# Moving the layer norm's root and two elementwise steps of a cross-attention loop from VectorE to GpSimd, folding the gate into Wo, with a new order of the pieces

## What is computed

```
x1 = x + tanh(g_xattn) * (attention(layernorm(x), ctx) @ Wo + bo)
x2 = layernorm(x1) = (x1 - mean) / sqrt(var + 1e-5)
S  = sigmoid(x2 @ Wg)             # 3584 tokens, 8 experts; each takes its top 896
out = x1 + tanh(g_ffn) * sum over experts of S * (gelu(x2 @ W1 + b1) @ W2 + b2)
```

## Time and profile before

| what | value |
|---|---|
| profiled execution | 894.2 us |
| span | 892.4 us |
| median of three runs | 895.79 us |
| TensorE, VectorE busy | 814.0 us (91%), 708.3 us (79%) |
| ScalarE, GpSimd busy | 571.2 us (64%), 286.0 us (32%) |
| mean granted TensorE clock | 0.961 |

### The profile page before, as it was taken

One profiled execution on the slowest core, in us unless ns is written; L12 is line 12 of the kernel. 1 busy time (PEld: TensorE's weight loads), 2 busy tenths in 40 slices (PEclk: granted clock), 3 DMA queues, 4 the chain that ended last, 5 costly groups with the idle time before them and its releaser, 6 DMA issues. The chain is left out here.

```text
span 892.4 us, 22315 instructions
## 1 busy us (share of the span) xinstructions
PE 814.0 (91%) x8336; PEld 667.8 (75%) x8336; DVE 708.3 (79%) x1900; ACT 571.2 (64%) x1251; POOL 286.0 (32%) x269
## 2 busy tenths in 40 slices
PE   5989999999999999999996118999999999999995
PEld 3555888888888888888775006989898988888885
DVE  6888999999999999999875784787676767764542
ACT  2655877787777777877664214847576675849470
POOL 4760111011111111110100603366465655644504
PEclk9999999999999999999998557999999999999998
DMA  7843666776676676666610304162525344453303
GB/s 190 196 93 89 153 157 153 169 180 155 151 184 152 157 165 165 173 154 150 160 33 29 106 1 134 44 153 50 135 54 136 58 130 102 97 131 67 38 6 41
DMA packets 96210, 104.62 MB, mean 117 GB/s; under 512 B 11744, under 2 KB 92272, under 8 KB 96112
## 3 DMA queue, kind: packets, MB, share of 16 engines
q1 hardware_dynamic: 84128, 88.50, 38.5%
q0 software_dynamic: 10752, 14.69, 9.6%
q10 hardware_dynamic: 1232, 0.12, 0.1%
HBM read 39.60 MB, written 14.68 MB: 61 GB/s over the span
## 5 line engine op out<-in xcount | busy, mean ns | idle before, releaser
L485 DVE TENSOR_REDUCE a_nm<-a_pS 112x1 f32<-112x375 f32 x342 | 177.3, 538 | 4.7 <-PE a_pS L791 4.1
L1772 PE MATMUL e_p<-w2hl,e_hh 128*128 128x512 f32 x440 | 156.9, 397 | 0.0
L725 POOL TENSOR_TENSOR a_kp<-a_k_rest,a_kp 128x375 bf16<-128x375 f32 x56 | 50.4, 900 | 323.7 <-ACT a_kp L326 323.7
L785 PEld LDWEIGHTS a_pT<-a_qst,a_kst 98*128 98x128 bf16 x1536 | 102.8, 99 | 40.8 <-issue 11.7
L785 PE MATMUL a_pT<-a_qst,a_kst 98*128 98x112 bf16 x1536 | 123.5, 212 | 1.7 <-ACT a_P L306 1.0
L1566 POOL DMA_INDIRECT out_dram<-e_y,e_idx x56 | 89.1, 1591 | 109.2 <-ACT e_y L1605 103.2
L1774 PE MATMUL e_p<-w2hl,e_hl 128*128 128x256 f32 x440 | 122.8, 279 | 0.0
L1652 DVE TENSOR_TENSOR e_hl<-e_hid,e_hh 128x384 fp32r<-128x384 f32 (+1 forms) x128 | 77.8, 623 | 47.3 <-ACT e_hh L1598 46.3
L306 ACT ACTIVATE a_room<-a_pT 128x448 f32<-128x448 f32 x192 | 96.7, 543 | 28.1 <-PE a_pT L785 27.8
L791 PE MATMUL a_pS<-a_kst,a_qst 96*112 96x375 bf16 x342 | 107.8, 334 | 3.4 <-DVE a_nm L485 3.0
L306 ACT ACTIVATE a_P<-a_pT 128x448 f32<-128x448 f32 x192 | 97.7, 546 | 9.4 <-PE a_pT L785 8.1
(11 more groups left out here) (247 smaller groups left out, 1688.9 us busy)
## 6 DMA issues: line engine op xcount, KB each, us to landing
a_kst<-a_kp SPq DMA_DIRECT2D x192, 192.0 KB, 3.6
w<-in_L_ffn_W_dram SPq DMA_DIRECT2D x16, 1024.0 KB, 6.8
a_qst<-a_qp SPq DMA_DIRECT2D x96, 112.0 KB, 3.0
a_craw<-in_ctx_dram SPq DMA_DIRECT2D x32, 128.0 KB
a_room<-in_x_dram SPq DMA_DIRECT2D x8, 448.0 KB, 6.6
a_xb<-in_x_dram SPq DMA_DIRECT2D x32, 112.0 KB, 3.4
out_dram<-a_x SPq DMA_DIRECT2D x32, 112.0 KB, 2.2
xn_scratch<-a_x SPq DMA_DIRECT2D x32, 112.0 KB, 2.2
```

Source lines behind the costliest of these rows:

```text
L485: dve.tensor_reduce(nm[:, h:h + 1], s_bank(b, h)[0:LQ, 0:LK], AXX, ALU.max, negate=True).then_inc(s_used, 1)
L785: last = pe.matmul(pT[u % 2][:, j * LQ:(j + 1) * LQ], kst[b % 4][:, h, c * 128:(c + 1) * 128], q_of(b, slice(None), h), start=True, stop=True)
L1772: pe.matmul(p2[g % 2][:], hh[:, f, rows], T.w2hl[r % 2][:, f].rearrange("p q d -> p (q d)"), start=(f == 0), stop=(f == 7), skip_group_che ...
```

## The change

* `added` now adds x plus bias, and writes x1 at once; `gated` is gone. tanh(g) is multiplied once into Wo and into bo, on GpSimd, before the loop.
* GpSimd adds bo to the reloaded x (`x_biased`), one batch ahead of its use; SP reloads x one batch earlier.
* VectorE keeps the statistics of x1 (`x1_statistics`, `x1_moments`). GpSimd takes the inverse root (`root`: a power with exponent -0.5, and two Newton steps, one column each), and the normalised x1 (`x2_of`).
* The bank of the Wo product is free with `x1_ready` instead of `wo_read`.
* The order of the pieces in all loops is new. Both `k_mid_part` of ScalarE are last in the step, the context is loaded for batch m+7 instead of m+8, and the last two key copies of SP stand behind the row of maxima.

```diff
+                dve.wait_ge(xb_ready, b + 1)
                 dve.wait_ge(wo_ready, b + 1)
-                dve.tensor_tensor(xo[:], pM[0][0:LQ, 0:D], bo[:], ALU.add).then_inc(wo_read, 1)
-            def gated(b):
-                dve.scalar_tensor_tensor(xo[:], xo[:], gx[0:LQ], xb[p][:], ALU.mult, ALU.add).then_inc(x1_ready, 1)
+                dve.tensor_tensor(xo[:], pM[0][0:LQ, 0:D], xb[p][:], ALU.add).then_inc(x1_ready, 1)
...
+            def x1_moments(b):
+                dve.wait_ge(ln, b + 1)
+                wait(dve, x2_ready, b - 1)
+                dve.bn_aggr(mv[b % 2][:], stats[:]).then_inc(mv_ready, 1)
...
+            def x_biased(b):
+                pool.wait_ge(xb_loaded[b % 2], 16 * (b // 2 + 1))
+                pool.tensor_tensor(xb[b % 2][:], xb[b % 2][:], bo[:], ALU.add).then_inc(xb_ready, 1)
+
+            def root(b):
+                pool.wait_ge(mv_ready, b + 1)
+                pool.tensor_scalar(ve[:], mv[b % 2][:, 1:2], EPS, None, ALU.add).then_inc(root_set, 1)
+                pool.tensor_scalar(nvh[:], mv[b % 2][:, 1:2], EPS, -0.5, ALU.add, ALU.mult).then_inc(root_set, 1)
+                pool.wait_ge(root_set, 7 * b + 1)
+                pool.tensor_tensor(y[:], ve[:], mhalf[:], ALU.pow).then_inc(root_set, 1)
+                for k in range(2):
+                    pool.wait_ge(root_set, 7 * b + 2 * k + 3)
+                    pool.tensor_scalar(yy[:], y[:], y[:], nvh[:], ALU.mult, ALU.mult).then_inc(root_set, 1)
+                    pool.wait_ge(root_set, 7 * b + 2 * k + 4)
+                    pool.tensor_scalar(y[:], yy[:], 1.5, y[:], ALU.add, ALU.mult).then_inc(root_set, 1)
+
+            def x2_of(b):
+                pool.wait_ge(root_set, 7 * b + 7)
+                pool.tensor_scalar(x2[b % 2][:], x1[b % 2][:], mv[b % 2][:, 0:1], y[:], ALU.subtract, ALU.mult)\
+                    .then_inc(x2_ready, 1)
+
+            pool.wait_ge(gx_ready, 1)
+            pool.wait_ge(bo_done, 1)
+            pool.tensor_scalar(bo[:], bo[:], gx[0:LQ], None, ALU.mult).then_inc(scaled, 1)
+            pool.tensor_scalar(wo[:], wo[:], gx[:], None, ALU.mult).then_inc(scaled, 1)
+            pool.memset(mhalf[:], -0.5).then_inc(scaled, 1)
+            pool.wait_ge(scaled, 3)
             for m in range(FIRST, LAST):
                 if live(m + 5, EARLY_K):
                     k_low_part(m + 5, 0)
                     k_low_part(m + 5, 1)
+                if live(m + 1):
+                    x_biased(m + 1)
+                if live(m):
+                    root(m)
+                    x2_of(m)
```

More of the change, by code:

```diff
@@ L105, in attention @@
         x2T = sb("x2T", [128, 2 * LQ])
-        stats, mv = sb("stats", [LQ, 6]), sb("mv", [LQ, 2])
+        stats, mv = sb("stats", [LQ, 6]), [sb(f"mv{i}", [LQ, 2]) for i in range(2)]
+        ve, mhalf = sb("ve", [LQ, 1]), sb("mhalf", [LQ, 1])
         nvh, y, yy = sb("nvh", [LQ, 1]), sb("y", [LQ, 1]), sb("yy", [LQ, 1])
@@ L266, in _ @@
                     stack_keys(m + 4, (2, 3))
-                if live(m):
-                    x_again(m)
+                if live(m + 5, 4):
+                    stack_queries((m + 5) // 2, (3, 4, 5) if (m + 5) % 2 else (0, 1, 2))
+                if live(m + 2, 1):
+                    row_max(m + 2)
+                if live(m + 1):
+                    x_again(m + 1)
                 if live(m + 4, 3):
                     stack_keys(m + 4, (4, 5))
[L271 to L276, removed]
                 if live(m - 1):
                     results(m - 1)
+                if live(m + 7, 6):
+                    context(m + 7)
             for p in range(2):
@@ L440, in _ @@
                     ct_copy(m + 6)
-                if live(m + 1):
-                    o_copy(m + 1)
+                if live(m + 5, EARLY_K):
+                    k_mid_part(m + 5, 0)
+                    k_mid_part(m + 5, 1)
         @block.vector
@@ L881, in wo_product @@
                 pe.wait_ge(cct_copied, b + 1)
+                if b == 0:
+                    pe.wait_ge(scaled, 2)
                 for k in range(2):
@@ L995, in _ @@
                     values(m + 2, 1)
+                if live(m):
+                    cc_transposes(m, m)
+                if live(m + 1):
+                    scores_t(m + 1, 6)
+                if live(m + 3, 2):
+                    scores_s(m + 3, 2)
                 if live(m + 5, EARLY_K):
@@ L1019, in _ @@
                     ct_transposes(m + 6)
+                if live(m - 1):
+                    x2_transposes(m, m - 1)
+                if live(m + 3, 2):
+                    scores_s(m + 3, 5)
+                    scores_s(m + 3, 6)
+                if live(m + 1):
+                    scores_t(m + 1, 9)
+                    scores_t(m + 1, 10)
                 if live(m + 3, 2):
                     scores_s(m + 3, 7)
-                if live(m + 3, 1):
-                    scores_s(m + 3, 8)
                 if live(m):
```

140 lines of the change are left out of this document (45 added, 95 removed).

## The result

The changed kernel takes 883.44 us (median of four executions, 882.86 to 883.61), the kernel before 896.26 on the same chip (893.86 to 897.25): a ratio of 0.986, interval 0.9839 to 0.988. The profiled execution took 883.38 us, its span 881.6.

A forecast was written before the change was run, and what follows sets the result against it. TensorE (99% busy) was taken to set the pace, VectorE (96%) making it wait. Loop -7.0, start -0.6, loop end +1.3 gave -6.3 us: 894.2 to 887.9, plus 1.6 makes 889.5; range 885.5 to 897.0.

The forecast's parts named there:

- I put the new period at 12.57: Attention loop: a batch falls from 12.82 to 12.57 us, gaining 28 x 0.25 = 7.0 us.
- The waits of 0.2: TensorE before row-maximum products: VectorE's lateness costs 0.21 us in an ordinary batch of 12.71, above 12.50 of work.
- the 0.07 that I let stand: TensorE in the loop: 0.07 us a batch, a third of the ordinary wait, remains because maxima and banks still alternate.
- Bounds 28 x 0.32 = 9.0: Loop of 28 batches: the most to be gained is 9.0 us, from 12.82 to TensorE's 12.50; the least is nothing.
- The median of before is 1.6 higher, which makes 889.5: Whole kernel: 1.6 us between the old profiled execution and the old median is added to 887.9.
- The end of the loop, +1.3: Last batch's path: root chain on GpSimd adds 1.8 us, the gate's removal saves about 0.5; bounds +0.2 and +3.
- The start, -0.6: Batch 1: T products begin after two rather than four row-maximum products, saving 0.6 us; bounds 0 and 1.3.
- VectorE at 75%: Loop: 80.5 us of VectorE work goes over 28 batches, from 344.4 to 263.9 busy, so it no longer bounds.
- The slow chain: Rival, chance 0.12: GpSimd's root and x2 exceed the 1.9 us slack before x2's transposes; example 907 us.
- The lock: Rival, chance 0.14: GpSimd's x2 blocks VectorE's maxima split up to 1.25 us, costing up to 5.6 us: 895.
- when x2 runs: Lock rival's place: x2 at about 7.0 to 8.2 us, as VectorE splits the maxima by cast and two-input subtraction.
- The new order leaves the ordinary waits: Rival, chance 0.16: only long batches shorten, 12.82 to 12.71, gaining 3.1 us in the loop: 893.4.

The follow-up runs named there:

- the early-reload kernel: The kernel before with one edit: x for the addition reloaded one batch earlier; 889.56 us, ratio 0.9948.
- the work alone with x first: New work on GpSimd and VectorE in the old order, with SP reloading x at the head of each iteration, before the key copies; 894.11 us, ratio 0.9999.
- one more x2 ahead: The changed kernel with x2 computed one extra time on GpSimd (1.24 us, spare buffer) ahead of x2; 888.96 us, ratio 0.9929.
- the order alone: The changed kernel's order and earlier reload of x, with gate, Newton steps and x2 left on VectorE; 902.32 us, ratio 1.0104.
- work alone: The kernel before's order with the change's work moved to GpSimd, x reloaded a batch ahead, second low key part after x2; 894.03 us, ratio 1.0008.

## Why the prediction was off

The miss is 889.5 - 883.44 = 6.1 us. Its parts, by the prediction's own steps:

* **"I put the new period at 12.57" (failed, 3.1 us).** This is the main one. The waits of 0.2 were right, the 0.07 that I let stand had no row behind it: with VectorE relieved and the new order none of the ordinary wait is left, in any of the 25 batches (25 x 0.066 = 1.7). Applying one period to all 28 was the other half: the last three are shorter (12.09 on average), 3 x 0.48 = 1.4. With the reload early and all else as before they already take 12.71, 12.05 and 12.05. "Bounds 28 x 0.32 = 9.0" was therefore no bound: the stretch gained 10.05. In the old order the relieved period is 12.55 and in the new one 12.50, so about 0.05 a batch belongs to the order.
* **"The median of before is 1.6 higher, which makes 889.5" (failed, 1.5 us).** The excess was carried over as if it belonged to the chip. The changed kernel's median lies 0.06 from its profiled execution. Long batches alone don't explain why executions differ: the early-reload kernel has none in its profile and differs by 4.6 us, the work alone with x first has ten and differs by 4.8. The start is one part: the second weighted sum comes at 94.4 to 95.8 us in the four traces of all runs whose granted clock was 1.00 up to there, and at 100.05 in the early reload's, which had 0.94 in its first 84 us. What else varies was not traced.
* **The end of the loop, +1.3 (measured +0.36).** The chain was right: from the moments' end (475.64) to x2 (479.86) it is 4.22, where 4.1 was forecast, and 2.3 before. Missing was the last Wo product, 2.02 before and 1.12 after. The stretches around it, before and after, in the columns of the earlier trace rows (the granted clock is the third from the end):

```profile
483.00:488.00 5.00, 3.35 (x10) 2.06 (x10) 1.98 (x7) 1.12 (x4) 0.00 (x0) 0.62 0.15 46
488.00:493.00 5.00, 1.50 (x6) 1.11 (x6) 3.89 (x13) 0.53 (x2) 0.00 (x0) 0.50 0.15 46
```

```profile
472.00:477.00 5.00, 2.45 (x10) 1.65 (x10) 2.68 (x5) 1.18 (x4) 1.14 (x4) 0.73 0.15 46
477.00:482.00 5.00, 1.46 (x6) 1.11 (x6) 0.54 (x3) 0.36 (x1) 2.44 (x5) 0.50 0.15 46
```

  0.50 is the level of 1.2 GHz. The clock fell ahead of that product in the one and behind it in the other. In the 10 us ahead TensorE was busy for 7.8 (473 to 483, before) and for 8.0 (462 to 472, after), at 1.00. It is seen again with one more x2 ahead (1.90) and not with the early reload (1.12). What sets its moment was not tried.
* **The start, -0.6:** -0.73 between the two profiled executions. But two more of the changed kernel reach the second weighted sum at 96.64 and 98.25, against 96.87 here, so the runs don't show that the start gained anything.
* **VectorE at 75% (failed, without effect on the time).** It is 83%: I subtracted 80.5 us of durations, and 55.3 went. A duration of VectorE overlaps the next instruction: in the rows of the order alone L519 lasts 0.51 and the next starts 0.43 later. Summed over the 28 batches, durations fell by 77.9 us and overlaps by 22.4.

The rivals. The slow chain: slack 1.61 where I had 1.9, the power 0.57 where I had 0.4, x2 1.24 as in its row of the prologue; it was 1.6 us from coming true. The price per batch beyond it is nearly as stated (0.97 for 0.87), but the end of the loop would have cost more than the 2.4 I gave it. The lock is real and as long as feared, but it bites the work in the old order (7 and 10 batches of 28), not the new. Its remark that VectorE is held "when x2 runs" is half right: in the old order five casts are held inside x2, in the new one only 0.05 us a batch and 0.16 in each of the last three; the two-input operations beside x2 hold longer. The Trainium skill (SBUF — State Buffer, SBUF: two separate sides) says that the lock is held for the whole instruction, for a VectorE operation with two SBUF inputs too. The trace of the changed kernel disagrees for L498 and x2: it began 0.61 into x2's 1.24 and took 0.17 to 0.18 in the 25 ordinary batches. "The new order leaves the ordinary waits" is refuted: it needs the relief, and with it removes them all.

What the prediction didn't see is that work and order depend on each other. It costed the work's effect on VectorE's totals, and the order as nearly neutral. In the runs the totals of work alone were fine (VectorE 282 of the 343 us from 97 to 440) and the kernel was no faster.

## What to carry over

When an engine is relieved, its pacing neighbour falls to its own floor; count that floor from rows without a wait, and leave no remainder without a row. Take the last batches apart: with less work the next engine sets their pace (1.6 us less work gave 0.5 here). Work moved to GpSimd beside VectorE can need a new order with it: look where GpSimd's operations, the two-input ones above all, will stand against VectorE's small ones. Carry no offset between one profiled execution and a median over to another kernel. Lay an ordinary and a long batch of one trace over each other: the first row that differs names the cause.

## What the hardware showed that was not expected

* VectorE's cast and its two-input subtraction of 112x16 are held to the end of a two-input operation of GpSimd (up to 0.99, and 1.62 to 1.68 for two in a row). GpSimd's one-input x2 with per-partition scalars (1.24) holds them only in part: in the changed kernel until 0.57 after its start, in the work alone until 0.97.
* In the work alone with x first, the trace's nanoseconds separate the cases. Where GpSimd's low part starts 0.038 to 0.060 us after the cast, or before it, the cast is held (nine batches), and where it starts 0.062 to 0.081 after, it is free (17). That the low part's start is itself a sign of who came first is not excluded.
* On one column GpSimd takes 0.57 us for the power and 0.19 to 0.34 for an operation with scalars, and about 0.1 us lies between dependent ones (302.30 to 302.41), not the 0.25 of the earlier trace rows.
